# The sums of the state weights go ahead of the decay sums for two of four head pairs in a gated-attention kernel

## The chip, the cores and the metric

The kernel runs on one core of a Trainium2 chip. The metric is the time of one execution on the device, in microseconds (us), as the median of a few executions. The core has five engines with a queue of instructions each: PE (matrix products; PEld is its loading of weights), DVE (vector work), ACT (activations and copies), POOL, and SP, which here issues transfers. They run side by side and wait for one another only through semaphores.

## The reference

32 sequences of 512 rows and 512 columns go through a gated cross-attention and then a mixture of experts. The change touches the attention alone:

```python
log_f = jax.nn.log_sigmoid(fg)
cs = jnp.cumsum(log_f, axis=-1)
log_D = where(mask, cs[..., :, None] - cs[..., None, :], -inf) + ig[..., None, :]
max_log_D = jnp.max(log_D, axis=-1, keepdims=True)
D = jnp.exp(log_D - max_log_D)
C = (qh @ kh.T) / sqrt(dh) * D
normalizer = jnp.maximum(abs(C.sum(-1)), exp(-max_log_D))
h = (C / (normalizer + EPS)) @ vh          # then a norm per head, and x + tanh(g) * h
```

q is the normed x, k and v are the context; 8 heads of 64 columns, `ig` and `fg` are gates. Each row of x then gets a second norm (`xfb`), and from that the router's logits for the experts.

## The kernel before, in words

**Tiling.** A sequence is cut into 4 chunks of 128 rows. Within a chunk the scores q·k are multiplied by the decays D; what comes from earlier chunks goes through a state S (64x65 for each head), which queries weighted by a decay (`qw`) read. Heads go in pairs: pair p is heads 2p and 2p+1, p from 0 to 3.

**Stages.** `attention` runs a software pipeline: turn i of a loop of NB + 2 = 34 turns works on sequences i-1 (transposes of q and k, gates), i-2 (scores, states, products), i-3 (norm per head) and i-5 (transposes of the second norm's rows). Each engine has that loop written out for itself. Program order in each engine's queue is all that sets the order; there is no scheduler. The second norm of sequence i-5 is thus there for turns 5 to 33 alone, 29 of them; sequence i-2 for turns 2 to 33, 32 of them.

**The PE steps that matter here**, with the line of their instruction: `turn` (L674, transposes of q or k), `turn_rows` (L683, transposes of `xfb`), `chunk_state` (L788, three chunks), `decays` (L760 masks in bf16, L765, L771: they sum the exponents of D for a pair in the tile EX), `widths` (L779, one matmul that sums the weights of the queries for a pair), `scores` (L749, tile QK), `product` (L805 and L810, tile A), `shift_gates` (L717), `turn_gates` (L733).

**Banks.** Transposes, widths and chunk states share four banks of PSUM, T[0], T[1] and the two halves of QK. The table in `iteration_fills` names the bank of each fill, and `fill` makes PE wait until the engine that reads the bank's last content has taken it. For the rows of sequence i-5 and the pairs 1 and 2 it says:

```python
("xfT", b5, 0, "act", 1),
("qw", b2, 1, "dve", 0), ("scores", b2, 1, None, None), ("xfT", b5, 1, "act", 1),
("xfT", b5, 2, "act", 0), ("q", b1, 2, "act", 2), ("k", b1, 2, "act", 3), ("q", b1, 3, "act", 1),
```

So both `turn_rows(b5, 0)` and `turn_rows(b5, 1)` fill T[1], and ACT's copy of the first frees the bank for the second.

**The other engines' steps around it.** ACT: `first_state` (L472), `second_norm` (L510, writes `xfb`, for which `turn_rows(b5, 0)` waits), `squares` (L489), `decay_factors` (L466, exponent of EX into C, waits for the last matmul of `decays`), `turned_rows` (L457, copies out the transposed rows). Its order in a turn, in short:

```python
first_state(b2); second_norm(b5, (2, 3)); squares(b3, 3)
decay_factors(b2, 1)
turned_rows(b5, 0); turned_rows(b5, 1)
```

DVE: `chunk_states` (L1048, writes S and frees the halves of QK for `scores(b2, 1)`), `weighted_queries` (L1039, reads what `widths` made), `weighted_scores` (L1030, C times QK).

Of the kernel before, what the change touches and what calls it, by code (L numbers as in the profile page):

```python
# [75 lines left out]
def spread(ap, axis, n):  # L76

    ap = ap.unsqueeze(axis)
    return ap.to_broadcast([n if i == axis else s for i, s in enumerate(ap.shape)])
# [9 lines left out]
def attention(nc, io, NB, dram, sm_all, tg, consts, stored, plan):  # L89
# [6 lines left out]
    with ExitStack() as ctx:  # L96
# [60 lines left out]
        def live(b):  # L157
            return 0 <= b < NB
# [36 lines left out]
        def fill(pe, kind, b, k):  # L195

            if ahead[kind, b, k]:
                pe.wait_ge(*ahead[kind, b, k])
            if (kind, b, k) in weighted:
                pe.wait_ge(*weighted[kind, b, k])  # L200
            return bank[kind, b, k]
# [46 lines left out]
        with nc.Block() as block:  # L248
# [410 lines left out]
            def _(pe):  # L659
# [8 lines left out]
                def turn(kind, b, c):  # L668

                    src, blocks = (q, None) if kind == "q" else (kraw, b % VBUF)  # L670
                    t = fill(pe, kind, b, c)
                    for j in range(TILES):
                        rows = q[:, j, :] if kind == "q" else kraw[:, b % VBUF, j, :]
                        mm = pe.transpose(t[:, j * P:(j + 1) * P], rows[:, c * P:(c + 1) * P], ident[:, :])  # L674
                    mm.then_inc(s["tfull"], 1)
# [62 lines left out]
                def scores(b, p):  # L738

                    g = PAIRS * b + p  # L740
                    if g:
                        pe.wait_ge(s["cc"], 2 * g)
                    for taken in cleared.get((b, p), ()):
                        pe.wait_ge(*taken)
                    for j in range(TILES):
                        jj = slice(j * P, (j + 1) * P)
                        for par in range(2):
                            r = slice(DH * par, DH * par + DH)
                            mm = pe.matmul(QK[:, par, jj], kT[r, b % 2, p, jj], qT[r, b % 2, p, jj], start=True, stop=True)  # L749
                    mm.then_inc(s["qk"], 1)  # L750

                def decays(b, p):

                    g = PAIRS * b + p
                    if g:
                        pe.wait_ge(s["dd"], g)
                    top, end = slice(0, DH), slice(DH, P)
                    for a, r, mask in ((0, top, (maskneg, maskswap)), (1, end, (maskswap, maskneg))):
                        for t, m in zip((top, end), mask):
                            pe.matmul(EX[t, a, :], identb[r, r], m[r, :], start=True, stop=False, skip_group_check=True)  # L760
                    if p == 0:
                        pe.wait_ge(s["rp"], b + 1)
                    for a, r in ((0, top), (1, end)):
                        ones_of = pick[r, p, :, :].rearrange("k a j -> k (a j)")
                        pe.matmul(EX[:, a, :], climb[r, b % 2, :], spread(ones_of, 2, P), start=False, stop=False, skip_group_check=True)  # L765
                    if p == 0:
                        pe.wait_ge(s["xm"], b + 1)
                    for par in range(2):
                        for a, r in ((0, top), (1, end)):
                            half = slice(a * 2 * P, (a + 1) * 2 * P)  # L770
                            mm = pe.matmul(EX[:, a, par * 2 * P:(par + 1) * 2 * P], sel[r, 2 * p + par, :], peaks[r, b % 2, half],  # L771
                                           start=False, stop=True, skip_group_check=True)
                            if par:
                                mm.then_inc(s["ee"], 1)

                def widths(b, p):

                    t = fill(pe, "qw", b, p)
                    pe.matmul(t[:, 0:SEQ - P], selP[:, 2 * p:2 * p + 2, :].rearrange("k a d -> k (a d)"), inner[:, b % 2, :], start=True, stop=True)\  # L779
                      .then_inc(s["tfull"], 1)  # L780
# [11 lines left out]
                def product(b, p):  # L792

                    g = PAIRS * b + p
                    pe.wait_ge(s["cc"], 2 * g + 2)
                    if p == 0:
                        wait_taken(pe, "st", b, TILES - 2)
                    wait_taken(pe, "qw", b, p)
                    if g:
                        pe.wait_ge(s["an"], g)  # L800
                    for j in range(TILES):
                        for par in range(2):
                            for a in range(2):
                                r = slice(DH * a, DH * a + DH)
                                mm = pe.matmul(A[r, par, j, 0:VW], C[:, 2 * (g % CRING) + par, j * P + DH * a:j * P + DH * a + DH],  # L805
                                               vc[:, b % 2, j, 2 * p + par, :], start=(j == 0), stop=(j == 0), skip_group_check=True)
                    for j in range(1, TILES):
                        for par in range(2):
                            r = slice(DH * par, DH * par + DH)
                            mm = pe.matmul(A[:, par, j, 0:VW], qw[r, g % 2, (j - 1) * P:j * P], S[r, j - 1, p, :],  # L810
                                           start=False, stop=True, skip_group_check=True)
                    mm.then_inc(s["af"], 1)

                for i in range(NB + 2):
                    b1, b2, b3, b5, b6 = i - 1, i - 2, i - 3, i - 5, i - 6

                    if live(b3):
                        product(b3, 3)
                    if live(b2):
                        widths(b2, 0)  # L820
                    if live(b1):
                        pe.wait_ge(s["q"], b1 + 1)
                        pe.wait_ge(s_cd[b1 % VBUF], 16 * (b1 // VBUF + 1))
                        for c in range(2):
                            turn("q", b1, c)
                            turn("k", b1, c)
                    if live(b2):
                        for j in range(TILES - 1):
                            chunk_state(b2, j)

                        decays(b2, 1)
                    if live(b5):
                        turn_rows(b5, 0)
                    if live(b2):
                        widths(b2, 1)
                        scores(b2, 1)
                    if live(b5):
                        turn_rows(b5, 1)
                    if live(b2):
                        product(b2, 0)  # L840
                    if live(b5):
                        turn_rows(b5, 2)
                    if live(b1):
                        turn("q", b1, 2)
                        turn("k", b1, 2)
                        turn("q", b1, 3)
                    if live(b6):
                        turn_logits(b6)
                    if live(b5):
                        turn_rows(b5, 3)  # L850
                    if live(b1):
                        turn("k", b1, 3)

                    if live(b2):
                        decays(b2, 2)
                        widths(b2, 2)
                        scores(b2, 2)
                    if live(b1):
                        gates(b1)
                    if live(b2):  # L860
                        product(b2, 1)
                    if live(b1):
                        if b1 == 0:
                            pe.wait_ge(s["prep1"], 1)
                        shift_gates(b1)

                    if live(b2):
                        decays(b2, 3)
                        widths(b2, 3)
                    if live(b1):  # L870
                        chunk_ends(b1)
                    if live(b2):
                        scores(b2, 3)
                    if live(b5):
                        logits(b5)
                    if live(b2):
                        product(b2, 2)
                    if live(b1):
                        decays(b1, 0)
                        scores(b1, 0)  # L880
                        turn_gates(b1)
# [971 lines left out]
```

## Time and profile before

| | |
|---|---|
| median of 3 executions | 3051.26 us (3048.56 to 3052.82) |
| profiled execution, span | 3051.6 us |
| attention in it | from the start to about 970 us, then the experts |
| PE, DVE, ACT, POOL busy, 400 to 600 us | 197.4, 186.5, 162.6, 149.7 us of 200 |
| granted PE clock there | 1.00 (of 2.4 GHz) |

The profiled execution is 0.3 us from the median, so sums against its span can be read as sums against the median. The views used further on are the stretches (busy time and clock in windows), the waits (who waited for whom), and the timeline (instructions in order of time; equal neighbours are merged, and an idle time of the engine stands in brackets with what ended it). PE's matmuls overlap, so the distance between two starts says more than the length shown.

### The profile page before, as it was taken

How to read it: one execution, taken by the hardware profiler on the slowest of the kernel's cores; microseconds unless marked ns; L12 is line 12 of the kernel's file. 1: busy time of each engine (PE TensorE's matmuls, PEld its weight loads, DVE VectorE, ACT ScalarE, POOL GpSimd, SP SyncE). 2: the span in 40 equal slices, each digit the busy share in tenths (PEclk: the TensorE clock that was granted, in tenths of full speed). 3: DMA queues.
4: the chain of work that ended last, by engine and by line, in shares of the span. 5: the costliest groups of instructions: out<-in, count | busy, mean ns of one | idle time of the engine just before them, and what ended most of it. 6: DMA issues, size and time to landing. Idle time of an engine off the chain costs nothing.

```text
span 3051.6 us, 60802 instructions
## 1 busy us (share of the span) xinstructions
PE 2948.7 (97%) x24708; PEld 2395.3 (78%) x24708; DVE 1819.7 (60%) x5124; ACT 1132.8 (37%) x2025; POOL 1065.5 (35%) x1029
## 2 busy tenths in 40 slices
PE   6999999999997599999999999999999999999998
PEld 5888888888886477777777877787787787778886
DVE  6999999999998645354454444444434445444332
ACT  5788788787886211121121121122112122112110
POOL 4777777777776311111122111121112112121111
PEclk9999999999998699999999999999999999999999
DMA  3243444434443412241242132232123214222121
GB/s 122 100 160 120 162 139 149 161 123 165 141 134 113 131 40 37 35 99 31 46 99 48 36 80 35 37 96 62 31 38 93 41 31 111 38 50 57 35 37 24
DMA packets 140575, 250.71 MB, mean 82 GB/s; under 512 B 31968, under 2 KB 31968, under 8 KB 140296
## 3 DMA queue, kind: packets, MB, share of 16 engines
q1 hardware_dynamic: 106296, 170.80, 17.2%
q0 software_dynamic: 28672, 67.65, 12.6%
q10 hardware_dynamic: 5328, 8.36, 0.9%
q8 instruction: 197, 3.23, 0.4%
q14 instruction: 82, 0.67, 0.1%
HBM read 137.23 MB, written 101.19 MB: 78 GB/s over the span
## 4 chain that ended last, share of the span: by engine, by line
PE 64%; DVE 1%; DMA 1%; issue 0%; ACT 0%; POOL 0%; ACTq 0%; DVEq 0%; POOLq 0%
PE DN L1729 32%; PE UP L1700 30%; PE TT L1673 1%; DMA w_raw<-in_L_ffn_W_down 1%; DVE c_hit L1392 0%; PE c_bank L1385 0%; DVE down_lo L1258 0%; PE c_bank L1369 0%; DVE c_hit L1413 0%; ACT z L1643 0%; DVE c_within L1408 0%; ACT down_hi L1252 0%; POOL out_x L1618 0%; DVE c_gained L1445 0%; DVE mid_lo L1761 0%
## 5 line engine op out<-in xcount | busy, mean ns | idle before, releaser
L1618 POOL DMA_INDIRECT out_x<-y,slots x128 | 208.5, 1629 | 1621.1 <-DVE y L1785 1621.1
L1643 ACT ACTIVATE z<-UP,bup 128x512 f32<-128x512 f32 (+1 forms) x352 | 240.8, 686 | 1085.6 <-PE UP L1700 1066.5
L1729 PE MATMUL DN<-down_hi,mid_hi 128*128 128x512 f32 x1408 | 570.8, 405 | 0.0
L1700 PE MATMUL UP<-xT_hi,up_lo 128*128 128x512 f32 (+1 forms) x1408 | 555.5, 395 | 0.0
L1700 PE MATMUL UP<-xT_hi,up_hi 128*128 128x512 f32 (+1 forms) x1408 | 553.5, 393 | 1.8 <-DVE xT_lo L1740 0.9
L1700 PE MATMUL UP<-xT_lo,up_hi 128*128 128x512 f32 (+1 forms) x1408 | 552.0, 392 | 0.0
L1729 PE MATMUL DN<-down_hi,mid_lo 128*128 128x512 f32 x1280 | 505.8, 395 | 0.0
L1729 PE MATMUL DN<-down_lo,mid_hi 128*128 128x512 f32 x1280 | 505.7, 395 | 0.0
L1759 DVE CAST mid_hi<-z 128x512 fp32r<-128x512 f32 (+1 forms) x352 | 151.2, 429 | 486.4 <-ACT z L1643 486.4
L1783 DVE TENSOR_TENSOR y<-DN,bdn 128x512 f32<-128x512 f32 x128 | 88.5, 692 | 432.3 <-PE DN L1729 419.5
L1700 PEld LDWEIGHTS UP<-xT_hi,up_hi 128*128 128x128 f32 (+1 forms) x1408 | 260.3, 185 | 67.5 <-ACT z L1643 2.8
L1700 PEld LDWEIGHTS UP<-xT_lo,up_hi 128*128 128x128 f32 (+1 forms) x1408 | 259.8, 185 | 67.6 <-issue 0.5
L1700 PEld LDWEIGHTS UP<-xT_hi,up_lo 128*128 128x128 f32 (+1 forms) x1408 | 259.9, 185 | 65.5 <-issue 0.5
L1729 PEld LDWEIGHTS DN<-down_hi,mid_hi 128*128 128x128 f32 x1408 | 266.5, 189 | 56.1
L1729 PEld LDWEIGHTS DN<-down_hi,mid_lo 128*128 128x128 f32 x1280 | 240.4, 188 | 58.2
L1729 PEld LDWEIGHTS DN<-down_lo,mid_hi 128*128 128x128 f32 x1280 | 241.1, 188 | 50.1
L1761 DVE TENSOR_TENSOR mid_lo<-z,mid_hi 128x512 fp32r<-128x512 f32 (+1 forms) x352 | 244.1, 693 | 12.1
L1627 ACT ACTIVATE xT_hi<-TT 128x512 fp32r<-128x512 f32 x126 | 68.3, 596 | 467.0 <-PE TT L1673 446.9
L233 POOL TENSOR_TENSOR nsb<-nsb,rr 128x512 f32<-128x512 f32 x125 | 127.0, 1049 | 215.2 <-DVE nn L973 215.2
L1030 DVE SCALAR_TENSOR_TENSOR C<-QK,C 128x512 f32<-128x512 f32 x256 | 164.7, 685 | 8.5 <-PE QK L749 6.5
L749 PE MATMUL QK<-qT,kT 64*128 64x128 f32 x2048 | 146.4, 282 | 13.2 <-DVE S L1048 12.1
L1597 POOL DMA_INDIRECT xg<-rows_scratch,slots x128 | 137.5, 1075 | 56.3 <-issue 38.1
(264 smaller groups left out, 4971.9 us busy)
## 6 DMA issues: line engine op xcount, KB each, us to landing
xs<-in_x SPq DMA_DIRECT2D x64, 512.0 KB, 3.7
kraw<-in_ctx SPq DMA_DIRECT2D x32, 1024.0 KB, 7.3
out_x<-xs SPq DMA_DIRECT2D x32, 1024.0 KB, 12.5
rows_scratch<-xfb SPq DMA_DIRECT2D x32, 1024.0 KB, 10.6
w_raw<-in_L_ffn_W_down SPq DMA_DIRECT2D x40, 512.0 KB, 4.4
w_raw<-in_L_ffn_W_up SPq DMA_DIRECT2D x16, 682.5 KB, 4.1
mid_hi<-mid_hi ACTq DMA_DIRECT2D x32, 86.0 KB
mid_lo<-mid_hi ACTq DMA_DIRECT2D x32, 84.0 KB
```

Source lines behind the costliest of these rows:

```text
L233: ins = eng.tensor_tensor(n, n, spread(scale[:, j, :], 2, DH), ALU.mult)
L749: mm = pe.matmul(QK[:, par, jj], kT[r, b % 2, p, jj], qT[r, b % 2, p, jj], start=True, stop=True)
L1030: dve.scalar_tensor_tensor(out=c, in0=QK[:, par, :], scalar=DH ** -0.5, in1=c, op0=ALU.mult, op1=ALU.mult)\
L1597: pool.indirect_dma_start(xg[:, t, :], None, rows_v, bass.IndirectOffsetOnAxis(ap=slots[:, 4 * n + t:4 * n + t + 1], axis=0)).then_inc(s_r ...
L1618: pool.indirect_dma_start(out_rows, bass.IndirectOffsetOnAxis(ap=slots[:, m:m + 1], axis=0), y[:, t, :], None, compute_op=ALU.add).then_in ...
L1627: act.activation(xT[0][:, c, :], turned(n, c)[:, :], ACT.Copy).then_inc(s["thi"], 1)
L1643: act.activation(z[0:r, k % 2, :], UP[k % 3][0:r, :], ACT.Silu, bias=bup[0:r, e // 2, f:f + 1]).then_inc(s["z"], 1)
L1700: mm = pe.matmul(UP[k % 3][0:r, :], weights.up[wa][:, c, f * P:f * P + r], xT[xa][:, c, :], start=first, stop=(c == CH - 1 and wa == 1))
L1729: mm = pe.matmul(DN[m % 2][:, :], lhs, rhs, start=first, stop=(f == FCH - 1 and lhs is parts[-1][0]))
L1759: dve.tensor_copy(mid[0][0:r, f, :], z[0:r, k % 2, :]).then_inc(s["hi"], 1)
L1761: dve.tensor_tensor(mid[1][0:r, f, :], z[0:r, k % 2, :], mid[0][0:r, f, :].bitcast(FP32), ALU.subtract)\
L1783: dve.tensor_tensor(y[:, t, :], DN[m % 2][:, :], bdn[:, e % 2, :], ALU.add).then_inc(s["yp"], 1)
```

## The change

For pair 1 the decay sums go behind the rows' first transposes and the widths; for pair 2 they go behind the widths. Pair 0 and pair 3 stay as they are (pair 3 has its widths between the decay sums and the ends of the gates). Nothing is added or removed.

```diff
@@ -828,11 +828,11 @@
                         for j in range(TILES - 1):
                             chunk_state(b2, j)
 
-                        decays(b2, 1)
                     if live(b5):
                         turn_rows(b5, 0)
                     if live(b2):
                         widths(b2, 1)
+                        decays(b2, 1)
                         scores(b2, 1)
                     if live(b5):
                         turn_rows(b5, 1)
@@ -852,8 +852,8 @@
                         turn("k", b1, 3)
 
                     if live(b2):
+                        widths(b2, 2)
                         decays(b2, 2)
-                        widths(b2, 2)
                         scores(b2, 2)
                     if live(b1):
                         gates(b1)
```

On PE, pair 1, a turn from 5 on: chunk states (L788), decay sums (L760 to L771), rows' transposes (L683), widths (L779), scores (L749). In these names T0 and T1 are the two T banks.

```order
 L788 MATMUL QK<-uv,kraw 64x65 x16
-L760 MATMUL EX<-maskneg,identb 64x512
-L760 MATMUL EX<-maskswap,identb 64x512 x2
-L760 MATMUL EX<-maskneg,identb 64x512
-L765 MATMUL EX<-pick,climb 128x512 x2
-L771 MATMUL EX<-peaks,sel 128x256 x4
 L683 MATMUL T1<-ident,xfb 128x128 x4
 L779 MATMUL T0<-inner,selP 128x384
+L760 MATMUL EX<-maskneg,identb 64x512
+L760 MATMUL EX<-maskswap,identb 64x512 x2
+L760 MATMUL EX<-maskneg,identb 64x512
+L765 MATMUL EX<-pick,climb 128x512 x2
```

The ten matmuls of the decay sums now stand behind the four transposes and the one of the widths, right ahead of the scores; the second set of transposes into T1 comes behind the scores as before.

On PE, pair 2 of the same turn, after the last transposes of k (L674):

```order
 L674 MATMUL QK<-ident,kraw 128x128 x4
-L760 MATMUL EX<-maskneg,identb 64x512
-L760 MATMUL EX<-maskswap,identb 64x512 x2
-L760 MATMUL EX<-maskneg,identb 64x512
-L765 MATMUL EX<-pick,climb 128x512 x2
-L771 MATMUL EX<-peaks,sel 128x256 x4
 L779 MATMUL T1<-inner,selP 128x384
+L760 MATMUL EX<-maskneg,identb 64x512
+L760 MATMUL EX<-maskswap,identb 64x512 x2
+L760 MATMUL EX<-maskneg,identb 64x512
+L765 MATMUL EX<-pick,climb 128x512 x2
```

Only the one matmul of the widths has changed its place. ACT's and DVE's rows are the same in both kernels.

## Rows read from the trace of the kernel before

**Rows 1.** Stretches: window, length, busy time of each engine, granted clock.

```profile
400.00:600.00 200.00, 197.40 (x3350) 167.88 (x3350) 186.48 (x529) 162.55 (x318) 149.69 (x152) 1.00 0.44 144
```

**Rows 2.** Waits, 130 to 942 us: us in total, times, longest.

```profile
PE QK L749 <- DVE S L1048: 10.8, 25, 1.1
...
PEld T L683 <- ACT xfb L510: 4.7, 27, 0.2
...
PEld T L674 <- ACT qT L450: 0.4, 1, 0.4
```

**Rows 3.** Timeline, 534 to 542 us: pair 1 of one turn.

```profile
536.79 0.39 ACT L472 ACTIVATE S<-T 128x260 f32<-128x260 f32 x1
...
537.08 1.51 ACT L510 ACTIVATE xfb<-xs,nn,rr 128x512 f32<-128x512 f32 x2
537.61 0.40 PE L760 MATMUL EX<-maskneg,identb 64*64 64x512 bf16 x1
...
537.96 1.74 DVE L1048 SCALAR_TENSOR_TENSOR S<-S,gb,QK 128x65 f32<-128x65 f32 x8
...
538.64 0.66 PE L683 MATMUL T<-ident,xfb 128*128 128x128 f32 x4
539.01 1.00 ACT L466 ACTIVATE C<-EX 128x1024 f32<-128x1024 f32 x1
...
539.05 0.42 PE L779 MATMUL T<-inner,selP 128*128 128x384 f32 x1
...
539.85 1.16 PE L749 MATMUL QK<-qT,kT 64*128 64x128 f32 x16 [0.38 <-DVE S L1048]
539.92 0.58 ACT L457 ACTIVATE xfT<-T 128x512 f32<-128x512 f32 x1
...
540.94 0.66 PE L683 MATMUL T<-ident,xfb 128*128 128x128 f32 x4
```

**Rows 4.** Timeline of PE, pair 0: decay sums straight ahead of scores.

```profile
529.54 0.40 PE L760 MATMUL EX<-maskneg,identb 64*64 64x512 bf16 x1
...
530.44 1.05 PE L749 MATMUL QK<-qT,kT 64*128 64x128 f32 x16
```

**Rows 5.** Timeline, pair 3: ACT waits for the decay sums.

```profile
523.83 0.40 PE L760 MATMUL EX<-maskneg,identb 64*64 64x512 bf16 x1
...
525.02 1.02 ACT L466 ACTIVATE C<-EX 128x1024 f32<-128x1024 f32 x1 [0.39 <-PE EX L771]
```

**Rows 6.** Timeline of PE: the widths of pair 0, then a transpose.

```profile
533.82 0.45 PE L779 MATMUL T<-inner,selP 128*128 128x384 f32 x1
534.10 0.60 PE L674 MATMUL T<-ident,q 128*128 128x128 f32 x4
```

**Rows 7.** Timeline, pair 2, and DVE's weighted scores of it.

```profile
545.34 0.60 PE L683 MATMUL QK<-ident,xfb 128*128 128x128 f32 x4
545.78 0.63 PE L674 MATMUL QK<-ident,kraw 128*128 128x128 f32 x4
546.34 0.40 PE L760 MATMUL EX<-maskneg,identb 64*64 64x512 bf16 x1
...
547.33 0.44 PE L779 MATMUL T<-inner,selP 128*128 128x384 f32 x1
547.70 1.16 PE L749 MATMUL QK<-qT,kT 64*128 64x128 f32 x16
...
551.10 1.28 DVE L1030 SCALAR_TENSOR_TENSOR C<-QK,C 128x512 f32<-128x512 f32 x2
```

**Rows 8.** Timeline, turn 33: the rows' second transposes after ACT's copy.

```profile
949.50 0.59 ACT L457 ACTIVATE xfT<-T 128x512 f32<-128x512 f32 x1
950.14 0.42 PEld L683 LDWEIGHTS T<-ident,xfb 128*128 128x128 f32 x4 [0.18 <-ACT xfT L457]
```

**Rows 9.** Stretches of 2 us, columns as in rows 1.

```profile
66.00:68.00 2.00, 1.70 (x35) 1.51 (x34) 1.80 (x8) 2.00 (x4) 0.00 (x0) 1.00 0.00 0
...
974.00:976.00 2.00, 0.00 (x0) 0.00 (x0) 1.73 (x11) 0.00 (x0) 0.00 (x0) 0.50 1.01 370
```

## The prediction

> **What bounds the kernel now.** I read the busy time in stretches first, then the waits, then the timeline of one turn piece by piece. The attention is a loop of 34 turns, and the change is in PE's order there; the experts behind it are not touched, so what the attention gains or loses is passed on whole. In the middle of the attention PE is busy 197.4 of 200 us at full clock, DVE 186.5, ACT 162.6 [rows 1]: PE is the bound, and its idle time is the only slack on the path. The waits say where that lies: PE waits 25 times for DVE's S ahead of the scores of pair 1, 10.8 us in all, 0.43 us each, and 27 times, 0.17 us each, for ACT's `xfb` ahead of the rows' transposes [rows 2]. Both waits are inside the piece that the change reorders. So the question is what PE did while others finished, and what it will do now.
>
> In the timeline of that piece [rows 3] the decay sums start at 537.61, straight behind the chunk states. ACT writes `xfb` from 537.08 to 538.59, and PE starts the rows' transposes at 538.64, 0.05 us behind it. The decay sums fill exactly the time in which `xfb` is made. S is done at 539.70, and the scores start at 539.85. ACT's exponent starts at 539.01, and its copy of the transposed rows lasts from 539.92 to 540.50, before PE wants the bank again at 540.94.
>
> **Pair 1, moved behind the rows and the widths (29 turns).** No instruction is added or dropped, so only the places count. Times are those of rows 3.
>
> - The rows' transposes still can't start before `xfb`, 538.64. Could `xfb` come earlier? ACT gets there from its copy of the first chunk state (536.79) without a gap, and that copy waits on PE work that the change leaves alone. So no. PE now idles from about 537.6 to 538.64, about 1.0 us where it had decay sums.
> - Widths at 539.05, as before.
> - Decay sums behind the widths: not in this trace as a pair. The next transpose follows widths by 0.28 us [rows 6]; going from transposes to the masks takes 546.34 - 545.78 = 0.56 where transposes follow one another by 0.44 (545.78 - 545.34) [rows 7], so 0.12 more for that change. I take 0.28 + 0.12 = 0.40: masks at 539.45. Bounds: 0.28 below (no extra), and above the 0.56 of transposes ahead of masks.
> - Scores: masks to scores without widths between them is 530.44 - 529.54 = 0.90 [rows 4], so 540.35. That is 0.50 later than 539.85, and the wait for S (539.70) is gone within it.
> - ACT's exponent: where ACT waits for the decay sums, it starts 525.02 - 523.83 = 1.19 us behind the masks [rows 5]: 540.64, instead of 539.01. Behind it on ACT is the copy of the transposed rows. From the exponent's start to the copy's it is 539.92 - 539.01 = 0.91, and the copy takes 0.58 [rows 3]: it ends at 542.13.
> - The second transposes of rows go into the same bank, T[1], and wait for that copy. Turn 33 shows this wait already: the copy ends at 950.09, PE goes on at 950.14 [rows 8]. So they start at 542.18. PE's own work would have had them at 540.35 + (540.94 - 539.85) = 541.44; the rest, 0.74 us, is a new wait.
> - Against 540.94 that is 1.24 us later, and everything behind it on PE moves along: products, transposes of q and k, pair 2. DVE's weighted scores, the next reader, wait for the exponent until about 541.6, but the product that needs them is itself moved by 1.24.
>
> Does it come back later in the turn? Only if PE waited for something there. After the two named, the longest wait of PE or its loads on another engine in that view is one of 0.4 us [rows 2], so no slack is left to eat it. DVE, ACT and POOL get about 1.2 us more idle time per turn.
>
> In turns 2 to 4 there are no rows to transpose; the scores of pair 1 then have the same work ahead of them in another order, and S still to wait for: nothing either way.
>
> **Pair 2, widths first (32 turns).** The widths fill T[1], which ACT frees by its copy of q's fourth block well before; the masks wait for an exponent long done. Before, from the last transposes to the scores: 547.70 - 545.78 = 1.92 us [rows 7]. Now 0.44 + 0.40 + 0.90 by the same pieces [rows 4, 6, 7] = 1.74. A gain of 0.18 us a turn. The exponent has to wait for masks at 545.78 + 0.84 = 546.62, so it starts at 547.81 and is done by 548.9; DVE reads it at 551.10 [rows 7], so that hides. Were the 0.40 the upper 0.56, the gain would be 0.02; at the lower 0.28 it would be 0.30.
>
> The Trainium skill, page "TensorEngine Tiling (Array Packing)", section on key properties, says that changing the tiling mode drains the engine. It speaks for the change: the new order changes shape twice between k's transposes and the scores of pair 2, the old one four times. By that rule alone both pairs would gain, which is the first rival; the trace agrees on pair 2 and sets two arrivals from ACT against it on pair 1.
>
> **Sum.** 1.24 - 0.18 = 1.06 us for 29 turns is 30.7; turns 2 to 4 take off 0.18 each, 0.5: **+30 us**. The profiled span of 3051.6 would be 3081.6; the median before is 0.3 less, so **3081 us**, 1.0% slower. With the bounds of the step from widths to masks the net is 0.82 (0.28: masks 0.12 earlier in both pairs takes 0.24 off) to 1.38 (0.56: 0.32 on), times 29: 24 to 40 us, so 3075 to 3091.
>
> **Rivals.**
>
> *Faster: shapes decide.* If ACT had `xfb` ready by 537.6 and the copy 0.2 us sooner, pair 1 would end where it ended, since S holds the scores anyway, and pair 2's 0.18 x 32 = 5.8 us would remain: **3045**. It decides once `xfb` ends a full 1.0 us earlier relative to the chunk states. For it: two of the 29 turns don't show PE's wait for `xfb`. Against it: the other 27 show the same 0.17 us [rows 2], and ACT's unbroken chain. Chance 0.06.
>
> *Slower by little: the bank wait doesn't form.* If ACT reached its copy in time, the scores alone would be late: 0.50 - 0.18 = 0.32 us, times 29, is 9: **3060**. Turn 33 speaks against it [rows 8], since there PE waits for the copy even with the decay sums early. Chance 0.08.
>
> *No change: what is lost is absorbed.* Were PE held elsewhere in the turn by DVE or ACT, by about 1 us, the new waits would replace that: **3051**. DVE is 93% busy [rows 1], which speaks for it a little; rows 2 speak against it. That the change doesn't do what it says is out: the order of PE's instructions shows both moves. Chance 0.03.
>
> *Much slower: the clock.* The clock is 1.00 where PE is busy 1.70 of 2 us, and at 0.50 in a stretch in which PE does nothing [rows 9]. The new gaps are about 1.0 and 0.74 us, in a piece of 5 us. If it fell to 1.2 GHz there each turn, some 3 us of work would take 3 more: 29 x 3 = 87 on top, **3168**. The Trainium skill, page "TensorE: Matmul & The Clock Gate", section "What's actually happening", says that the throttled state is the default and activity releases it; nothing in the rows shows it lost over gaps as short as these. Chance 0.03.
>
> **How the numbers follow.** The forecast has what is left of 1, 0.80. The range takes the forecast with its bounds, reaches down to the case without the bank wait, and has 3 us at the top for a further wait: 3059 to 3094. A measurement of this kernel tells about 0.2%, 6 us, from no change. Faster: 0.05 (the gain of 6 is at the edge). Same: 0.05. Slower: 0.90.
>
> **What would show it.** In the profile after, PE waits for `xfb` ahead of L683 by about 1 us in each of 29 turns, then for the copy L457 ahead of the second L683 by 0.7 us; the wait for S is gone; ACT's exponent of pair 1 waits for L771 by over 1 us; a turn takes about 1.06 us more; from k's last transposes to the scores of pair 2 it is 1.74 us instead of 1.92; the clock stays at 1.00. I would be wrong if `xfb` followed the chunk states sooner, if the second transposes started straight behind the scores, or if the end of the attention didn't move with them.

## The result, and the profile after

The changed kernel takes 3084.69 us (3078.58 to 3088.01, 4 runs) against 3052.04 us (4 runs) for the kernel before on the same chip: a ratio of 1.0097, 95% interval 1.0085 to 1.0109. The forecast was 3081, in a range of 3059 to 3094.

| | before | after |
|---|---|---|
| span of the profiled execution | 3051.6 us | 3086.3 us |
| first product of the experts (end of the attention) | 1041.0 us | 1070.8 us |
| PE busy, 400 to 600 us | 197.40 us | 189.45 us |
| one turn, mean of 26 from 150 us on | 29.27 us | 30.26 us |
| one turn, the middle one (median) of these 26 | 29.16 us | 30.22 us |

The end of the attention moved by 29.8 us, which is what the sum was about. The other 4.9 us between the two spans lie in the experts, which are the same code: from their first product to the end it is 2010.6 us before and 2015.5 after, and between 2009.5 and 2015.5 in the profiles of the study. In the chain of waits PE is held at some places by the loading of `W_down`, three places in the one execution, five in the other. That does not explain the 4.9 us: in "rows last" (below) there are five such places too, and its experts take 2010.1 us. What makes them vary stays open. I therefore read each experiment twice, by its time, and by the start of the experts.

The mean of a turn is not the whole story either. In some turns PE stands still for up to about 1 us without waiting for anything that the profile shows (it calls this `issue`), and the next turns then run unevenly. In the execution before, 6 of the 26 turns are more than 0.2 us above the middle one, in the one after only 1. The middle turn is therefore the fairer measure of what an order of instructions costs, and the table below gives both.

The waits of the changed kernel, 130 to 975 us (total us, times, longest), answer to [rows 2]:

```profile
PEld T L683 <- ACT xfb L510: 29.6, 27, 1.1
PE T L683 <- ACT xfb L510: 25.9, 27, 1.0
...
PEld T L683 <- ACT xfT L457: 18.5, 28, 1.0
POOL uv L388 <- DVE tm L1020: 16.8, 27, 0.6
...
PE T L683 <- ACT xfT L457: 13.2, 28, 0.8
```

The wait for `xfb` is now 1.10 us a turn on PE's loads where it was 0.17; the wait for ACT's copy `xfT` is new, 0.66 us a turn; PE's wait for S is gone from this list. A third line is new and was not in the forecast: POOL waits for DVE's `tm` in 27 turns.

The same piece of a turn as [rows 3], in the timeline of the changed kernel:

```profile
551.15 1.51 ACT L510 ACTIVATE xfb<-xs,nn,rr 128x512 f32<-128x512 f32 x2
...
552.71 0.66 PE L683 MATMUL T<-ident,xfb 128*128 128x128 f32 x4 [0.96 <-ACT xfb L510]
552.75 1.74 DVE L1048 SCALAR_TENSOR_TENSOR S<-S,gb,QK 128x65 f32<-128x65 f32 x8
553.12 0.42 PE L779 MATMUL T<-inner,selP 128*128 128x384 f32 x1
...
553.48 0.40 PE L760 MATMUL EX<-maskneg,identb 64*64 64x512 bf16 x1
...
554.64 1.16 PE L749 MATMUL QK<-qT,kT 64*128 64x128 f32 x16
554.66 1.02 ACT L466 ACTIVATE C<-EX 128x1024 f32<-128x1024 f32 x1 [1.49 <-PE EX L771]
555.58 0.59 ACT L457 ACTIVATE xfT<-T 128x512 f32<-128x512 f32 x1
...
556.23 0.65 PE L683 MATMUL T<-ident,xfb 128*128 128x128 f32 x4 [0.42 <-ACT xfT L457]
```

Read it as a chain. `xfb` is done at 552.66, the transposes start at 552.71. The exponent starts 554.66 - 553.48 = 1.18 us behind the masks, the copy 0.92 behind the exponent, it ends at 556.17, and the second transposes start 0.06 later, 3.52 us behind the first. Before it was 2.30. The scores start 1.16 us behind the masks, not 0.90: S is done at 554.49 and comes 0.26 too late. That last one was not forecast.

### The profile page after: what moved, and what is told of

Same layout as the page of the kernel before. It is cut to its first block, busy times and chain, and to the rows that moved or that the text cites. A ratio compares the mean times of both kernels' runs of the same rounds, so it can differ in the third digit from the quotient of the medians.

```text
span 3086.3 us, 60802 instructions
## 1 busy us (share of the span) xinstructions
PE 2947.0 (95%) x24708; PEld 2394.5 (78%) x24708; DVE 1838.2 (60%) x5124; ACT 1141.9 (37%) x2025; POOL 1063.8 (34%) x1029
## 4 chain that ended last, share of the span: by engine, by line
PE 62%; DMA 2%; DVE 2%; issue 0%; ACT 0%; POOL 0%; ACTq 0%; DVEq 0%; POOLq 0%
PE DN L1729 31%; PE UP L1700 29%; DMA w_raw<-in_L_ffn_W_down 2%; PE TT L1673 1%; DVE c_hit L1392 0%; DVE down_lo L1258 0%; PE c_bank L1385 0%; ACT z L1643 0%; PE c_bank L1369 0%; DVE c_hit L1413 0%; DVE mid_lo L1761 0%; DVE c_within L1408 0%; ACT down_hi L1252 0%; POOL out_x L1618 0%; DVE mid_hi L1759 0%
## 5 line engine op out<-in xcount | busy, mean ns | idle before, releaser
L466 ACT ACTIVATE C<-EX 128x1024 f32<-128x1024 f32 x128 | 130.7, 1021 | 66.2 <-PE EX L771 62.6
```

Source lines behind the costliest of these rows:

```text
L466: act.activation(C[:, first:first + 2, :].rearrange("t r (a n) -> t r a n", a=2), EX[:, :, :].rearrange("t a (r n) -> t r a n", r=2), ACT. ...
```

## The experiments

The steps are compared by distances between starts on PE, means over 26 turns from 150 us on, worked out from each run's timeline. "xfb step" is from the first chunk state (L788) to the rows' first transposes, "to scores" from these to the scores of pair 1, "to second" from the scores to the second transposes, "pair 2" from the first q transposes behind product 0 to the first gates matmul. "Turn" is from one first chunk state to the next: the mean, and the middle one of the same 26.

| run | time, ratio to before | experts start | turn, mean | turn, middle | xfb step | to scores | to second | pair 2 |
|---|---|---|---|---|---|---|---|---|
| before | 1 | 1041.0 | 29.27 | 29.16 | 2.58 | 1.24 | 1.09 | 4.87 |
| changed | 1.0097 | 1070.8 | 30.26 | 30.22 | 2.58 | 1.90 | 1.61 | 4.57 |
| pair 1 alone | 1.0108 | 1073.8 | 30.38 | 30.36 | 2.58 | 1.75 | 1.76 | 4.87 |
| pair 2 alone | 0.9985 | 1038.4 | 29.25 | 28.97 | 2.58 | 1.38 | 1.09 | 4.57 |
| copy first | 1.0020 | 1050.0 | 29.57 | 29.41 | 2.58 | 1.69 | 1.00 | 4.57 |
| late xfb | 1.0141 | 1082.1 | 30.75 | 30.72 | 3.10 | 1.66 | 1.85 | 4.57 |
| probabilities later | 1.0083 | 1068.2 | 30.17 | 30.07 | 2.58 | 1.70 | 1.81 | 4.57 |
| rows last | 0.9973 | 1035.1 | 29.01 | 28.96 | 2.91 | 0.95 | 1.10 | 4.57 |
| states first | 1.0238 | 1108.0 | 31.72 | 31.65 | 2.58 | 0.76 | 1.16 | 4.59 |
| states and copy first | 1.0247 | 1116.6 | 31.94 | 31.66 | 2.58 | 0.76 | 1.09 | 4.65 |
| one sum later | 0.9961 | 1025.4 | 28.80 | 28.70 | 2.58 | 0.86 | 1.10 | 4.59 |
| rows last, one sum later | 0.9968 | 1028.4 | 28.82 | 28.71 | 2.93 | 0.60 | 1.17 | 4.57 |

(In the two runs with "rows last" the widths and the decay sums are part of the xfb step.)

### Each move alone

The first leaves pair 2 as before, the second pair 1.

```diff
 # pair 1 alone, against the changed kernel
-                        widths(b2, 2)
                         decays(b2, 2)
+                        widths(b2, 2)
                         scores(b2, 2)
```

> The move of pair 1 alone; pair 2 as before. Theory (two waits for ScalarE on pair 1, a saved change of array shape on pair 2): 29 turns of +1.24 us = +36 us against the kernel before, about 3088, which is 5 to 6 us above the changed kernel; the experts start at about 1077 us in the profile. Rival (the whole loss is one of DVE's lateness or of both moves together): about the time of the changed kernel, 3082 to 3085, or below it.

Measured: 3088.18 us, ratio 1.0108 (1.0091 to 1.0124). The attention ends 32.8 us later than before, and 3.0 later than in the changed kernel. All the loss is pair 1's; the theory of two waits stands, with 33 us where I had 36. The middle turn is 1.20 us longer, where the forecast had 1.24.

```diff
 # pair 2 alone, against the changed kernel
+                        decays(b2, 1)
                     if live(b5):
                         turn_rows(b5, 0)
                     if live(b2):
                         widths(b2, 1)
-                        decays(b2, 1)
```

> The move of pair 2 alone; pair 1 as before. Theory: 0.18 us less in each of 32 turns, 5.8 us less than before: about 3046, and from the last transposes of k to the scores of pair 2 it is 1.74 us instead of 1.92. Rival (the time saved is waited away further down the turn): 3052, and the turns as long as before.

Measured: 3048.89 us, ratio 0.9985 (0.9976 to 0.9994). The time is 5.6 us below the median of the kernel before on that chip (3054.5), where 5.8 were forecast; by the ratio it is 4.6. The middle turn is 0.19 us shorter (28.97 against 29.16), where the theory had 0.18. That it fits so well is in part luck: the pair 2 step is shorter by 0.30 us, more than forecast, because the gates behind the scores start 0.11 sooner as well, and in the middle turn the scores of pair 1 start 0.09 later again. PE's wait for S, 130 to 942 us, has grown:

```profile
PE QK L749 <- DVE S L1048: 14.7, 26, 1.1
```

That is 0.57 us a turn where it was 0.43 [rows 2]. Part of what pair 2 gives, DVE's S takes.

The mean turn hides the gain, since it is shorter by only 0.02. In this execution 11 of the 26 turns are more than 0.2 us above the middle one, against 6 in the one before. Three stops of PE without a wait that the profile shows stand among them, 0.51 to 1.04 us long:

```profile
460.00 0.69 PE L805 MATMUL A<-vc,C 128*64 128x65 f32 x16 [0.91 <-issue]
```

The time of this profiled execution, 3051.72 us, is also the longest of the 11. A single profile can lead astray in the other direction too: turn 4's transposes of the gates (L733) start at 120.2 us instead of 122.7, but 1.9 of these 2.5 us are there at the widths of pair 1 in turn 2 (44.79 against 46.69), before an instruction of pair 2 has run. The rival (the time saved is waited away further down the turn) is right for about a third of the 0.30 us, not for all of it.

### The two waits apart

ACT copies the rows' first transposes out before it takes the exponent. Nothing else in the changed kernel is touched.

```diff
                     if live(b2):
+                        if live(b5):
+                            turned_rows(b5, 0)
                         decay_factors(b2, 1)
                     if live(b5):
-                        turned_rows(b5, 0)
                         turned_rows(b5, 1)
```

> The changed kernel, with ScalarE copying the first transposed rows before it takes the exponent of pair 1, so that the bank is free early. Theory: the second rows' transposes no longer wait (0.42 to 0.47 us in each of 28 turns in the trace of the changed kernel) and start 1.09 us behind the scores: 0.5 us a turn less, 14.5 us, about 3070. If my predicted 0.74 us were right (scores not held by S), 21 us less, 3063. Rival (the first wait alone costs all, the bank wait is covered): no change, 3085.

Measured: 3060.54 us, ratio 1.0020 (1.0011 to 1.0029), and the attention ends 20.8 us sooner than in the changed kernel. The timeline shows the copy in a gap that ACT had while it waited for the decay sums:

```profile
543.27 0.66 PE L684 MATMUL T<-ident,xfb 128*128 128x128 f32 x4 [0.96 <-ACT xfb L510]
543.96 0.60 ACT L457 ACTIVATE xfT<-T 128x512 f32<-128x512 f32 x1 [0.22 <-PE T L684]
544.92 1.05 PE L750 MATMUL QK<-qT,kT 64*128 64x128 f32 x16
545.21 1.02 ACT L466 ACTIVATE C<-EX 128x1024 f32<-128x1024 f32 x1 [0.66 <-PE EX L772]
545.91 0.66 PE L684 MATMUL T<-ident,xfb 128*128 128x128 f32 x4
```

(PE's lines are one further down in this file.) The second transposes follow the first by 2.64 us instead of 3.52. From the means it is 2.69 instead of 3.51, 0.82 us a turn. I had told this run's theory with 0.5 us, from the wait shown in the changed kernel; the prediction's own figure of 0.74 was nearer. The wait shown was the smaller one because S was late there and held the scores; both were running side by side, and in this run S is in time again.

Then the other wait, made longer: in the changed kernel ACT takes its squares first and makes `xfb` behind them.

```diff
-                    if live(b5):
-                        second_norm(b5, (2, 3))
                     if live(b3):
                         squares(b3, 3)
+                    if live(b5):
+                        second_norm(b5, (2, 3))
```

> The changed kernel, with ScalarE's squares of the pair before ahead of the norm that makes xfb: xfb comes 0.52 us (squares 0.62, less some overlap) later in each of 29 turns. Theory: the arrival of xfb sets the turn, so all of it shows: +15 to +18 us, about 3101. Rival (DVE's S or the exponent's own chain sets the turn): +0 to +5 us.

Measured: 3097.35 us, ratio 1.0141 (1.0125 to 1.0156), 11 to 13 us above the changed kernel by time and by the experts' start.

```profile
PEld T L683 <- ACT xfb L510: 43.7, 27, 1.7
```

The wait grows from 1.10 to 1.62 us a turn, the xfb step by 0.52, and from the first to the second transposes it stays at 3.51. So a later `xfb` passes into the turn, which grows by 0.50 in the middle one; 29 turns of that would be 14.5 us, not far from the 11 to 13 measured. The 15 to 18 us expected took the squares with 0.6 us and 29 turns.

### DVE's lateness

In the changed kernel's timeline DVE's last product of the probabilities takes 1.07 us:

```profile
545.94 1.19 POOL L246 TENSOR_TENSOR xs<-xs,nsb 128x512 f32<-128x512 f32 x1
546.11 1.07 DVE L942 TENSOR_TENSOR sm_all<-ex,sx 128x32 f32<-128x32 f32 x1
547.10 0.33 DVE L1019 COPY gb<-T 64x8 f32<-64x8 f32 x2
```

Its median is 1068 ns after and 191 ns before. In the kernel before it starts just ahead of POOL's addition instead of behind it:

```profile
532.19 0.19 DVE L942 TENSOR_TENSOR sm_all<-ex,sx 128x32 f32<-128x32 f32 x1
532.23 1.20 POOL L246 TENSOR_TENSOR xs<-xs,nsb 128x512 f32<-128x512 f32 x1
```

This run puts the probabilities behind the copies of the turned gates.

```diff
-                    if live(b6):
-                        probabilities(b6)
                     if live(b1):
                         turned_gates(b1)
+                    if live(b6):
+                        probabilities(b6)
```

> The changed kernel, with VectorE's probabilities (whose last product takes 1.07 us instead of 0.19 in the changed kernel's trace) behind the copies of the turned gates instead of ahead of them. Theory (the second transposes are held by ScalarE's copy, so that VectorE's lateness is mostly covered): the scores of pair 1 start 0.2 us sooner, the second transposes still 3.5 us behind the first; 0.12 us a turn less ahead of the chunk states, 3 us in all, about 3082. Rival (VectorE's lateness is what makes the change slow): 10 us or more less, under 3075.

Measured: 3079.96 us, ratio 1.0083 (1.0069 to 1.0096). The attention ends 2.6 us sooner than in the changed kernel. The scores start 0.20 us sooner, the second transposes do not: 1.70 + 1.81 = 3.51. The middle turn is 0.15 shorter, ahead of the chunk states: from the widths of pair 0 to the first chunk state the middle one is 2.24 us again, as before, where it was 2.39 in the changed kernel. DVE's lateness is real and costs about 3 us of the 30; the rest of it is covered by ACT's copy.

### Orders that keep the cover

If the decay sums were the cover for `xfb`, widths can still go ahead of them as long as the rows come last. The line of the bank table moves too.

```diff
-                        decays(b2, 1)
+                        widths(b2, 1)
+                        decays(b2, 1)
                     if live(b5):
                         turn_rows(b5, 0)
                     if live(b2):
-                        widths(b2, 1)
                         scores(b2, 1)
...
-  ("st", b2, 2, "dve", 3), ("xfT", b5, 0, "act", 1),
-  ("qw", b2, 1, "dve", 0), ("scores", b2, 1, None, None), ("xfT", b5, 1, "act", 1),
+  ("st", b2, 2, "dve", 3), ("qw", b2, 1, "dve", 0),
+  ("xfT", b5, 0, "act", 1), ("scores", b2, 1, None, None), ("xfT", b5, 1, "act", 1),
```

> Pair 1 with widths, then decay sums, then the rows' first transposes (its line in the table of banks moved too), then scores; pair 2 as in the change. The decay sums cover the making of xfb again. Theory: no wait of 1 us for xfb, the exponent and the copy come about as early as before, and the wait for S ahead of the scores holds as before; so it runs like the kernel with pair 2 moved alone: 3049, 5 us less than before. Rival (reading the state weights early is itself what costs on pair 1): 15 to 30 us slower than before.

Measured: 3047.02 us, ratio 0.9973 (0.9963 to 0.9984): faster than both kernels. The rows' transposes come 0.33 later, but then the scores only 0.95 behind them. The middle turn of 28.96 us is that of pair 2 alone (28.97), as the theory had it, and the intervals of the two times overlap: reading the state weights early on pair 1 costs nothing as long as `xfb` keeps its cover, and the rival is out. PE still waits for S in 25 turns:

```profile
PE QK L749 <- DVE S L1048: 8.0, 25, 0.6
```

Two attempts to take that wait away followed, both on the order of DVE before S. The first moves the sums over heads (2.28 us) behind the states, in the kernel before with pair 2 moved:

```diff
-                    if live(b1):
-                        head_sums(b1)
                     if live(b2):
                         chunk_states(b2)
+                    if live(b1):
+                        head_sums(b1)
```

> The kernel before, with pair 2 moved, and VectorE making the states S ahead of its sums over heads (2.28 us) instead of behind them. Theory (the wait for S, about 0.6 us a turn once pair 2 is moved, is what ate the gain of pair 2 in the steady turns): scores of pair 1 start 0.8 us behind the rows' transposes instead of 1.4, the second transposes then wait for ScalarE's copy until 1.9 us behind the first instead of 2.5: 0.58 us less in each of some 29 turns, 17 us less than with pair 2 alone, about 3032. Rival (PE is not held by S; or the sums over heads are needed as early): no change against pair 2 alone, 3049, or more.

Measured: 3125.01 us, ratio 1.0238 (1.0221 to 1.0256). The place itself does what was expected: scores 0.76 us behind the rows instead of 1.38. Yet the mean turn is 2.47 us longer. DVE now waits where it had worked, and is missed later on:

```profile
DVE S L1048 <- PE QK L788: 42.8, 27, 1.8
...
PEld T L779 <- DVE rise L1065: 27.8, 26, 1.2
```

42.8 us over 27 turns is 1.6 us a turn of DVE waiting for the chunk states. By pair 3 it is so late that PE waits up to 0.97 us for its `rise`, and in most turns the clock goes there:

```profile
555.70 0.45 PE L779 MATMUL T<-inner,selP 128*128 128x384 f32 x1 [0.97 <-DVE rise L1065]
556.36 0.59 PE L724 MATMUL T<-ends,later 128*128 128x8 f32 x2 [0.21 <-DVE ends L1068]
556.81 0.57 PE L725 MATMUL T<-unseen,ident 128*128 128x4 f32 x2
557.30 2.08 PE L749 MATMUL QK<-qT,kT 64*128 64x128 f32 x16
559.31 1.93 PE L692 MATMUL T<-xfT,Wr 128*32 128x128 f32 x32
```

The scores take 2.08 us, and the logits 1.93, where they are 1.16 and 1.08 elsewhere. Stretches of 1 us give the granted clock (third number from the end):

```profile
555.00:556.00 1.00, 0.30 (x1) 0.19 (x1) 0.93 (x3) 1.00 (x4) 1.00 (x2) 1.00 0.00 0
556.00:557.00 1.00, 0.79 (x4) 0.64 (x4) 0.74 (x3) 1.00 (x2) 1.00 (x2) 0.50 0.08 16
```

From 556 to 562 us PE runs at 1.2 GHz. From the shift of the gates (L717) to the scores of pair 3 the middle turn takes 3.61 us instead of 2.13, and from there to the scores of pair 0 it takes 6.47 instead of 4.90. These 3.05 us are more than the whole loss; 0.54 come back at the scores of pair 1.

Not all of it is the clock. In 20 of 27 turns the scores and the logits show the low clock, and such turns last 31.6 to 33.1 us. In the other 7 it stays at 1.00, in one of them behind the same wait of 0.97 us:

```profile
208.10 0.44 PE L779 MATMUL T<-inner,selP 128*128 128x384 f32 x1 [0.97 <-DVE rise L1065]
...
209.30 1.16 PE L749 MATMUL QK<-qT,kT 64*128 64x128 f32 x16
210.39 1.08 PE L692 MATMUL T<-xfT,Wr 128*32 128x128 f32 x32
```

The turns with the full clock take 29.8 to 30.4 us, 0.8 to 1.4 more than the middle one with pair 2 alone: that is the price of DVE's lateness by itself. The clock adds 1.5 to 3 us in a turn in which it falls.

The same with ACT's copy first, as above, on top:

> As the run with the states first, and ScalarE's copy of the first transposed rows ahead of the exponent of pair 1. Theory: the second transposes then start straight behind the scores, about 1.8 us behind the first instead of 1.9: 0 to 4 us less again, about 3030, as long as the later exponent does not hold the product. Rival: the later exponent makes VectorE late, and it gets 5 to 15 us slower than the run with the states first.

Measured: 3130.49 us, ratio 1.0247 (1.0233 to 1.0261), against 1.0238: no gain, and not clearly worse; the middle turn is the same (31.66 and 31.65). Its clock is 0.92 between 400 and 600 us. The copy was not what held this kernel, so the run says nothing on the copy.

The second attempt moves only 0.68 us of DVE's work, one sum of squares, behind the states:

```diff
-                    if live(b3):
-                        square_sums(b3, 2)
                     if live(b1):
                         head_sums(b1)
                     if live(b2):
                         chunk_states(b2)
                     if live(b3):
+                        square_sums(b3, 2)
                         square_sums(b3, 3)
```

> The kernel before with pair 2 moved, and VectorE making only one of its three sums of squares (0.68 us, pair 2 of the sequence before) behind the states S instead of ahead of them; its sums over heads stay ahead. Theory (S holds the scores of pair 1, and VectorE had no idle time in front of S until more than 1.6 us of work was taken from there): S and the scores come 0.6 us sooner, 0.8 us behind the rows' transposes; the second transposes then wait for ScalarE's copy, 1.9 us behind the first instead of 2.5; VectorE does the same work without a gap: up to 0.58 us a turn less than pair 2 alone, 3032 to 3040. Rival (any work taken from in front of S is missed later on VectorE, as in the run with the states first, where DVE was late and PE's clock fell to 1.2 GHz for some 5 us a turn): no gain, or slower than 3049, with the clock below 1.00 between 400 and 600 us.

Measured: 3040.64 us, ratio 0.9961 (0.9948 to 0.9975), the lowest time of the study, just above the theory's 3032 to 3040, with the attention 15.6 us shorter than before. There is a gain and the clock stays at 1.00, so the rival is out. PE is busy all of the time and DVE more than before:

```profile
400.00:600.00 200.00, 199.97 (x3405) 170.94 (x3403) 191.26 (x538) 164.61 (x321) 151.30 (x155) 1.00 0.46 150
```

The scores come 0.86 us behind the rows. The second transposes come 1.10 behind the scores, 1.96 behind the first, where ACT's copy was to hold them until 1.9. The middle turn is 0.27 us shorter than with pair 2 alone, not 0.58: of the 0.47 gained at the scores, 0.21 are lost from the shift of the gates to the scores of pair 3 (2.34 us instead of 2.13 in the middle turn), so DVE is a little late there too.

On top of "rows last" the same move:

> The kernel with the rows' transposes last (widths, decay sums, rows, scores), and the same one sum of squares behind the states. Theory: the wait for S there (0.32 us in 25 turns) goes, and nothing else holds the second transposes: 0.3 us a turn less, about 9 us, 3038. Rival as before: no gain, 3047, or slower with a lower clock.

Measured: 3042.22 us, ratio 0.9968 (0.9957 to 0.9979), with a middle turn of 28.71 us, as in the run before (28.70): the two orders do not add up. The 0.25 us a turn against "rows last" show in the trace; the times of these two overlap in their intervals.

## Why the prediction was right, point by point

**The turn: right.** The middle turn grew by 30.22 - 29.16 = 1.06 us, where the sum had 1.06. The terms below say how much of that is luck.

**`xfb` holds the rows' transposes: shown.** Same 2.58 us from the first chunk state to the rows in every run in which ACT keeps its order and no more than the decay sums stand between the two, 1.1 us of waiting a turn after the change, and a delay of `xfb` of 0.52 us came out as 0.50 on the turn. Where the decay sums are put back as the cover ("rows last"), the loss is gone.

**ACT's copy holds the second transposes: shown.** 0.42 us in the timeline, 0.82 us a turn when it is taken away. The forecast had 0.74.

**The step of 0.40 us from widths to masks** measured 553.48 - 553.12 = 0.36; the exponent's 1.19 measured 1.18; first to second transposes 3.54 measured 3.52. The rows at hand for each pair of neighbours were enough.

**"The wait for S is gone": wrong, without consequence.** From the start of `xfb` on ACT to the end of S it is 554.49 - 551.15 = 3.34 us where it was 539.70 - 537.08 = 2.62 [rows 3]: S came 0.7 us later, while DVE lost about 0.9 us on one instruction. I had taken DVE's distance to PE as fixed. The scores were held 0.2 us by it; the copy held longer, so the sum did not feel it.

**Pair 1, +1.24 us a turn:** in the middle turn it is 1.21 more from the first to the second transposes, and the turn of "pair 1 alone" grows by 1.20. Its attention ends 32.8 us later; 36 were forecast. The 29 turns would give 35; but the execution before had more uneven turns, 2.9 us of them in all against 0.5, and started its loop later, and that makes the difference to it smaller.

**Pair 2, -0.18 us a turn:** up to the scores it is 562.79 - 561.06 = 1.73 us in the changed kernel, 1.74 forecast. The gates behind start 0.11 sooner, which was not in the sum. So pair 2 gives 0.30. Against that, 0.15 us are lost ahead of the chunk states in the changed kernel, which was not in the sum either: DVE's product takes 1.07 us there, 0.74 in "pair 1 alone", and with "probabilities later" the 0.15 are gone. These two, 0.12 too little gain and 0.15 of a loss left out, cancel. The terms 1.21 - 0.30 + 0.15 make 1.06; that the total hits the forecast to the hundredth is luck, while the two large terms are understood. "S and its wait" stood in the forecast for pair 1; that the same wait would take about a third of pair 2's gain when pair 2 moves alone did not.

**"About 1.2 us more idle time per turn" for DVE:** wrong, without consequence. From the busy times between 400 and 600 us, ACT's idle time grew by about 1.1 us a turn, DVE's by only about 0.3, since its product took 0.9 us longer.

**The rivals.** "Shapes decide" is borne out for PE alone at pair 2, where two changes of shape fewer go with 0.30 us less; for pair 1 no run shows it apart. It is not what the turn goes by. Its "two of the 29 turns" without a wait for `xfb` was a misreading: the window of [rows 2] holds 28 of the 29. "No bank wait" is what the run with the copy first makes: +9.0 us by the end of the attention and +6 by time, and 9 was the figure given; its terms were not those of the forecast, since pair 2 gave 0.30 and another 0.2 us went to a wait for DVE at pair 3. The clock stayed at 1.00 in the changed kernel, as expected, though gaps of 0.96 us came every turn.

## What to carry to other kernels

Work that looks free to move on the bound engine may be the cover for another engine's result: before moving it, look at when the next instruction's input arrives, and read the short waits (here 0.17 us) as "arrives just in time", not as "nearly free". A move also shifts the order in which the other engines get their inputs, so follow it to the next reuse of the same buffer. And where an engine is 93% busy, take a little work from in front of a late result, not a lot: 0.68 us moved gave 13 us against the same kernel without it, 2.28 us moved cost 70 (experts' start 1025.4 and 1108.0 against 1038.4; by the ratios of the times, 7 and 77). And where single turns are uneven, compare the middle turn of many, not the mean of one profile: the mean would have hidden the gain of pair 2 altogether.

## What the runs showed of the hardware that was not expected

**A DVE product of 0.19 us that takes 1.07 us.** DVE's product starts 0.17 us behind POOL's addition and ends with it (545.94 + 1.19 = 547.13, and 546.11 + 1.07 = 547.18, in the timeline shown with that run). Its median is 191 ns before. The Trainium skill, page "SBUF — State Buffer", section "SBUF: two separate sides", says that VectorE with two inputs from SBUF and GpSimd share a pair of ports as an exclusive lock, held for the whole instruction by whichever comes first. Here both inputs are in SBUF, and the trace agrees for DVE: in the changed kernel, and in "pair 1 alone" (median 738 ns), the product starts behind POOL's addition in turn after turn and ends about 0.05 us behind its end. In the kernel before it starts 0.04 us ahead (532.19 and 532.23) and takes 0.19. That POOL waits when it comes second is not shown: its addition takes 1.20 us there and 1.19 in the changed kernel. A shift of 0.2 us between the engines decided it, in most turns. The product waits for no semaphore of POOL's in its code, and the profile shows the wait as a long instruction, not as idle time; so engines do not wait for one another through semaphores alone, as I wrote at the start.

**A clock that falls around a gap of 1 us, in most turns.** In "states first", with a gap of 0.97 us and small products behind it (widths, and the four of L724 and L725), the granted clock went from 1.00 to 0.50 and stayed there until 562 us. It did so in 20 of 27 turns; the mean between 400 and 600 us was 0.93. In one of the other 7 the gap was 0.97 us as well. The changed kernel has a gap of 0.96 us too, between full work, and its clock stays at 1.00. So the length of the gap alone does not decide it; what does is not shown. I had called a falling clock over such gaps unlikely (0.03). It did not happen in the kernel that I forecast, but it is a real price, (2.08 - 1.16) + (1.93 - 1.08) = 1.8 us on the scores and the logits alone in the turn shown, in a kernel with much the same gap in another place.

What stays open: whether "one sum later" is held by the copy or by DVE at the second transposes, since both come within 0.1 us, which was not tried apart; and what makes PE stop for up to 1 us in some turns and the experts vary by 6 us from one execution to another.
